# The second head group's square on the other two quadrants of TensorE's array, in turn with the first group's cube

## The chip, the cores and the metric

One core of a Trainium2 chip runs the whole kernel. The metric is the device time of one execution in microseconds (us). The array of TensorE (PE in the profile) has 128 rows and 128 columns; a matmul with a 64x64 stationary operand uses one quadrant of it: its rows are the SBUF partitions of its operands (0 to 63 or 64 to 127), its columns the PSUM partitions of its output. DVE is VectorE, ACT is ScalarE, POOL is GpSimd.

## What is computed

Six stages run over x of 32 batches x 256 tokens x 128, each as x + stage(layernorm(x)): a LoRA feed-forward, linear attention, the feed-forward again, an FP4 feed-forward, Nystrom attention, the FP4 feed-forward again. The change is in the Nystrom stage alone, which computes for each batch and each of 16 heads of 8 dimensions, with 64 landmarks:

```python
kernel1 = softmax(Q @ K_l.T); kernel2 = softmax(Q_l @ K_l.T); kernel3 = softmax(Q_l @ K.T)

def iterative_inv(mat, n_iter=6):
    K = mat
    V = K.T / max(column sums of K)
    for _ in range(n_iter):
        KV = K @ V
        V = (0.25 * V) @ (13 * I - KV @ (15 * I - KV @ (7 * I - KV)))
    return V

out = ((kernel1 @ iterative_inv(kernel2)) @ (kernel3 @ V)) @ w_proj
```

## The kernel before

Each engine runs its own list of instructions in the order in which the program wrote it, and semaphores are the only link between engines. The function `nystrom` writes, for each of the four engines, a loop over blocks: block n holds the six Newton steps of batch n (`run`) and, between them, parts of the batches before it (`tail`, n - 1) and after it (`head`, n + 1, and `fore`, n + 2). The order within a block is written out by hand. Two buffers (`s`, `o`) alternate.

The iteration is kept as a symmetric 64x64 matrix `pm` per head with 8 more columns that carry the product with kernel3 @ V, so that a step is a square and a cube. The 16 heads of a batch lie as 8 pairs: one head of a pair on partitions 0 to 63, the other on 64 to 127. Pairs 0 to 3 are group 0 and pairs 4 to 7 group 1; in PSUM (`pn`) each group fills one bank. For each step `it` and group `g`:

- `multiply` (PE, L1620): 8 matmuls, 64x64 by 64x72, write the square of `pm` to `pn`. The two heads of a pair use the two quadrants on the array's diagonal.
- `square` (ACT, L1378): one instruction copies the group's square, scaled, from `pn` to `sq` in SBUF.
- `remainder` (DVE, L1199): 7 pm - square, with the square read from `pn`, goes to `rm`. POOL's `remainder` (L1471) subtracts `sq` from `pm` into `tm`.
- `cube` (PE, L1630): 8 matmuls of `rm` by `sq` write the product over the square in `pn`, on the same diagonal quadrants.
- `newton` (DVE, L1207): the next `pm` from `pn` and `tm`. In the last step only the 8 extra columns are formed.

Every float32 matmul leaves two MATMUL and two LDWEIGHTS records in the trace, so a group of 8 matmuls is x16 there.

The work between the steps on PE: `turned1` (L1654, L1659), `scores2` (L1540), `back` (L1670), `scores3` (L1553), `turn2` (L1562), `product` (L1680), `totals` (L1690), `turn3` (L1570, four times a block), `columns` (L1576), `project` (L1697), `factors` (L1580), `start_w` (L1590), `turn_w` (L1598), `scores1` (L1640), `turn_x` (L1515), `queries` and `values` (L1522 to L1528), `turn_mx` (L1648) and `start_p` (L1612). `start_p` forms the first `pm` of the next batch: 16 matmuls, 64x64 by 64x64, that go round all four quadrants of the array in turn. DVE also runs row maxima (`max3` L1151, `max1` L1225, `max2` L1136), reciprocals (`invert` L1232), `divide` (L1237) and others; ACT runs the exponentials (`exp3`, L1360) and copies. Where a function is named with numbers, as newton(3,1), they are step and group; turn3(0) is its quarter.

## Time and profile before

| | us |
|---|---|
| median of 3 runs | 2293.45 |
| lowest and highest | 2290.79, 2293.51 |
| the profiled execution, its device time | 2292.12 |
| its span, first to last instruction | 2290.4 |
| the Nystrom stage, its steps L1620 to L1207 | 1052.3 to 2008.2 |

Busy time over the whole span: PE 1966.3 us (86%), PE's weight loads 1526.7, DVE 1718.3 (75%), ACT 1014.1, POOL 707.7. A row of groups gives an engine's instructions of one line: how many, their busy time (overlaps counted once), the mean time of one, and how long the engine sat idle before them, with the one that ended the idle time. Matmuls are pipelined: a group's own time in a row reaches to the end of its last matmul, while the next group starts earlier. The distance between the starts of two rows is therefore what the first one costs the engine.

### The profile page before, as it was taken

What the parts mean: (1) busy time and instruction counts of PE and PEld (TensorE: products, weight loads), DVE (VectorE), ACT (ScalarE), POOL (GpSimd) and SP (SyncE); (2) the same over time, 40 slices, a digit from 0 to 9 for tenths busy, and PEclk for the clock granted to TensorE, in tenths of its full rate; (3) what the DMA queues carried; (4) which work ended last, traced back from release to release, by engine and by line L of the source; (5) the groups of instructions that cost most, each with busy time, mean ns of one, the idle gap of its engine ahead of it and who ended that gap; (6) DMA issues with size and microseconds to landing.
All of it is one profiled execution on the core that took longest, in us unless ns stands there. A gap on an engine that the chain in (4) does not pass through costs nothing.

```text
span 2290.4 us, 66040 instructions
## 1 busy us (share of the span) xinstructions
PE 1966.3 (86%) x27657; PEld 1526.7 (67%) x27657; DVE 1718.3 (75%) x4007; ACT 1014.1 (44%) x2652; POOL 707.7 (31%) x835
## 2 busy tenths in 40 slices
PE   1999888888899677768999999999999999957775
PEld 0888555555688455546778778878887787735553
DVE  5666687787666699975777777777777777669995
ACT  1443222222344454444555555555555555345552
POOL 1000566666000122213333333333333333312221
PEclk9999999999999899988999999999999999979997
DMA  3000000000000000000000000000000000000002
GB/s 105 1 1 1 1 1 1 2 1 2 1 2 1 1 1 1 1 1 2 3 3 3 3 3 3 3 3 3 3 3 3 3 3 3 3 1 0 1 1 74
DMA packets 14551, 14.42 MB, mean 6 GB/s; under 512 B 1392, under 2 KB 12080, under 8 KB 14256
## 3 DMA queue, kind: packets, MB, share of 16 engines
q1 hardware_dynamic: 14256, 10.20, 1.6%
q8 instruction: 220, 3.60, 0.6%
q14 instruction: 75, 0.61, 0.1%
HBM read 6.01 MB, written 4.19 MB: 4 GB/s over the span
## 4 chain that ended last, share of the span: by engine, by line
PE 66%; DVE 21%; POOL 5%; ACT 4%; issue 3%; SPq 0%; DVEq 0%; POOLq 0%; DMA 0%
PE acc L1630 9%; PE acc L1620 9%; PE acc L467 6%; PE acc L444 5%; POOL arena L924 4%; DVE arena L888 3%; DVE arena L881 3%; PE acc L740 3%; PE acc L758 3%; DVE arena L891 3%; ACT arena L937 3%; PE acc L1654 2%; PE acc L458 2%; DVE arena L879 2%; PE acc L1640 2%
## 5 line engine op out<-in xcount | busy, mean ns | idle before, releaser
L1471 POOL TENSOR_TENSOR arena<-arena 128x288 f32<-128x288 f32 (+1 forms) x384 | 266.4, 708 | 484.8 <-ACT arena L1378 484.8
L924 POOL TENSOR_TENSOR arena<-arena 128x960 f32<-128x960 f32 (+2 forms) x70 | 118.1, 1687 | 577.3 <-DVE arena L891 571.8
L1199 DVE SCALAR_TENSOR_TENSOR arena<-arena,acc 128x256 f32<-128x256 f32 x384 | 160.7, 419 | 132.5 <-ACT arena L1378 121.1
L1620 PE MATMUL acc<-arena 64*64 64x72 f32 x6144 | 248.7, 227 | 1.0 <-DVE arena L1207 1.0
L1620 PEld LDWEIGHTS acc<-arena 64*64 64x64 f32 x6144 | 211.2, 133 | 56.4 <-issue 36.8
L1378 ACT ACTIVATE arena<-acc 128x288 f32<-128x288 f32 x384 | 157.9, 412 | 197.7 <-PE acc L1620 182.2
L1630 PE MATMUL acc<-arena 64*64 64x72 f32 x6144 | 241.1, 222 | 3.7 <-DVE arena L1199 3.5
L1630 PEld LDWEIGHTS acc<-arena 64*64 64x64 f32 x6144 | 208.7, 133 | 42.3 <-issue 27.2
L1207 DVE SCALAR_TENSOR_TENSOR arena<-acc,arena 128x288 f32<-128x288 f32 (+1 forms) x384 | 154.8, 410 | 68.4 <-PE acc L1630 57.8
L993 PE MATMUL acc<-wguT,arena 128*128 128x352 f32 x256 | 116.2, 540 | 60.7 <-DVE arena L863 57.2
L419 ACT ACTIVATE arena<-acc,wib 128x256 f32<-128x256 f32 x256 | 100.5, 475 | 150.5 <-PE acc L458 150.5
L1015 PE MATMUL acc<-wdT,arena 128*128 128x128 f32 (+1 forms) x768 | 105.7, 288 | 71.1 <-ACT arena L952 70.4
L662 POOL TENSOR_TENSOR arena<-arena,quadcol 128x512 f32<-128x512 f32 x64 | 65.3, 1042 | 289.9 <-DVE arena L539 289.9
L1015 PEld LDWEIGHTS acc<-wdT,arena 128*128 128x128 f32 (+1 forms) x768 | 93.2, 195 | 86.5 <-ACT arena L952 86.5
L565 DVE TENSOR_TENSOR arena<-acc,tri 128x512 f32<-128x512 f32 x192 | 120.6, 683 | 31.3 <-PE acc L740 31.3
L637 ACT COPY arena<-acc 128x512 f32<-128x512 f32 x64 | 37.6, 588 | 234.2 <-PE acc L740 234.2
L1360 ACT ACTIVATE arena<-acc,arena 128x256 f32<-128x256 f32 x256 | 119.5, 476 | 43.7 <-DVE arena L1151 43.7
L467 PEld LDWEIGHTS acc<-wout,arena 128*128 128x128 f32 x1024 | 119.1, 191 | 22.1 <-issue 22.1
L467 PE MATMUL acc<-wout,arena 128*128 128x128 f32 x1024 | 131.3, 281 | 1.2 <-DVE X L377 1.2
L444 PE MATMUL acc<-arena,wi 128*128 128x256 f32 x512 | 125.2, 389 | 0.0
L942 ACT ACTIVATE arena<-acc 128x352 f32<-128x352 f32 x128 | 58.3, 455 | 131.0 <-PE acc L993 131.0
L937 ACT ACTIVATE arena<-arena 128x960 f32<-128x960 f32 (+2 forms) x70 | 65.5, 935 | 108.8 <-DVE arena L881 108.6
(233 smaller groups left out, 4429.9 us busy)
## 6 DMA issues: line engine op xcount, KB each, us to landing
out_dram<-X SPq DMA_DIRECT2D x4, 1024.0 KB, 9.3
wi<-in_wiT_dram SPq DMA_DIRECT2D x1, 256.0 KB, 2.7
wout<-in_woT_dram SPq DMA_DIRECT2D x1, 256.0 KB, 3.3
wqkv<-in_w_qkv_dram SPq DMA_DIRECT2D x1, 192.0 KB, 2.7
arena<-in_w_down_dram SPq DMA_DIRECT2D x1, 176.0 KB, 2.3
arena<-in_w_gate_dram SPq DMA_DIRECT2D x1, 128.0 KB, 2.1
arena<-in_w_up_dram SPq DMA_DIRECT2D x1, 128.0 KB, 2.3
wq<-in_WqT_dram SPq DMA_DIRECT2D x1, 64.0 KB, 2.2
```

What stands on the lines that cost most here:

```text
L444: pe.matmul(hp[f], wi[:, f * P:(f + 1) * P], xnT[s], start=True, stop=False, skip_group_check=True)
L467: mm = pe.matmul(yp[s][:, j, :], hid[s][:, f, j * P:(j + 1) * P], wout[:, f, :], start=(f == 0), stop=(f == FT - 1), skip_group_check=True)
L565: dve.tensor_tensor(att[s][:, j * NQ + q, :].rearrange("p (h q) -> p h q", q=P), A[q].rearrange("p (h q) -> p h q", q=P), tri[:, 0:P].unsq ...
L924: pool.tensor_tensor(b3(zq[s][:, cols]), b3(rnd[s][:, cols]), each(small[s][:, 1, blocks(n)]), ALU.mult).then_inc(zq_ready, 1)
L937: act.activation(big[s][:, part(n)], y[s][:, part(n)], ACT.Abs, scale=2.0 ** 22)\
L1015: mm = pe.matmul(yp[:, j, :], hqT[s][j][0:w, c, :], wdT[0:w, c, :], start=(c == 0), stop=(c == HT - 1), skip_group_check=True)
L1199: dve.scalar_tensor_tensor(rm[s][:, group[g], :], pm[s][:, group[g], 0:LM], 7.0 * size[it], pn[s][:, group[g], 0:LM], ALU.mult, ALU.subtra ...
L1207: dve.scalar_tensor_tensor(pm[s][:, group[g], cols], pn[s][:, group[g], cols], 1.0 / (15.0 * size[it] ** 2), tm[s][:, group[g], cols], ALU ...
L1378: act.mul(sq[s][:, group[g], :], pn[s][:, group[g], 0:MW], 15.0 / (13.0 * size[it]))\
L1471: pool.tensor_tensor(tm[s][:, group[g], cols], pm[s][:, group[g], cols], sq[s][:, group[g], cols], ALU.subtract).then_inc(tm_ready, 1)
L1620: mm = pe.matmul(pn[s][rows, p, 0:MW], pm[s][rows, p, 0:LM], pm[s][rows, p, :], start=True, stop=True, skip_group_check=True)
L1630: mm = pe.matmul(pn[s][rows, p, cols], rm[s][rows, p, :], sq[s][rows, p, cols], start=True, stop=True, skip_group_check=True)
```

## The change

**Off the diagonal.** Group 1's square is now written to the other half of the partitions: a matmul whose operands lie on partitions 0 to 63 writes to 64 to 127, and the other way round. So it uses the two quadrants off the diagonal. Group 0's square and both cubes stay on the diagonal.

**In turn.** A new function `cross` issues, for p = 0 to 3, the two matmuls of group 0's cube for pair p and then the two of group 1's square for pair 4 + p. `multiply` is left for group 0 and `cube` for group 1. `cross` waits for what both need: `sq` and `rm` of group 0, `pm` of group 1.

**Back in two halves.** ACT copies group 1's square to `sq` with two instructions of 64 partitions each, each to the half where the head belongs. DVE's remainder of group 1 reads the square from `sq` instead of from `pn`, with other factors.

**New order.** All four lists are written anew, so that group 1 runs half a step behind group 0. `scores2` and `max2` move into the next block, ACT's `norm` is issued for n + 3 instead of n + 4. One semaphore for DVE's internal chains replaces one per stage.

```diff
+                    square, lead = (pn[s], 7.0 * size[it]) if g == 0 else (sq[s], 105.0 / 13.0)
+                    dve.scalar_tensor_tensor(rm[s][:, group[g], :], pm[s][:, group[g], 0:LM], lead,
+                                             square[:, group[g], 0:LM], ALU.mult, ALU.subtract).then_inc(rm_ready, 1)
...
+                    part = 1.0 / (15.0 * size[it] ** 2) if g == 0 else 13.0 / (225.0 * size[it])
...
                 def square(n, s, it, g):
                     act.wait_ge(sq_done, step(n, it, g))
-                    act.mul(sq[s][:, group[g], :], pn[s][:, group[g], 0:MW], 15.0 / (13.0 * size[it]))\
-                       .then_inc(sq_ready, 1)
+                    part = 15.0 / (13.0 * size[it])
+                    if g == 0:
+                        ins = act.mul(sq[s][:, group[g], :], pn[s][:, group[g], 0:MW], part)
+                    else:
+
+                        for (rows, _), (other, _) in zip(halves, halves[::-1]):
+                            ins = act.mul(sq[s][rows, group[g], :], pn[s][other, group[g], 0:MW], part)
+                    ins.then_inc(sq_ready, 1)
...
+                def cross(n, s, it):
+
+                    cols = slice(LM if it == NITER - 1 else 0, MW)
+                    pe.wait_ge(sq_ready, step(n, it, 0))
+                    pe.wait_ge(rm_ready, step(n, it, 0))
+                    iterate(pe, n, it, 1)
+                    for p in range(PG):
+                        for rows, _ in halves:
+                            mm = pe.matmul(pn[s][rows, p, cols], rm[s][rows, p, :], sq[s][rows, p, cols],
+                                           start=True, stop=True, skip_group_check=True)
+                        if p == PG - 1:
+                            mm.then_inc(cube_done, 1)
+                        r = PG + p
+                        for (rows, _), (other, _) in zip(halves, halves[::-1]):
+                            mm = pe.matmul(pn[s][other, r, 0:MW], pm[s][rows, r, 0:LM], pm[s][rows, r, :], start=True,
+                                           stop=True, skip_group_check=True)
+                    mm.then_inc(sq_done, 1)
```

PE's list after it, in a full block, is: multiply(0), turned1, scores2, cube(5,1) of the batch before, cross(0), back, scores3, multiply(1), cube(0,1), product, turn3(0), cross(1), totals, multiply(2), turn3(1), cube(1,1), turn2, turn3(2), cross(2), turn3(3), project, multiply(3), columns, cube(2,1), start_w, cross(3), factors, turn_w, multiply(4), scores1, cube(3,1), turn_x, cross(4), queries, values, multiply(5), turn_mx, start_p, cube(4,1), turned1, cross(5).

The first place is PE from `scores1` on, late in a block. Before, in the names above: scores1, cube(4,0), turn_x, multiply(4,1) with multiply(5,0), queries, values:

```order
L1640 MATMUL acc<-arena 128x256 x8
L1630 MATMUL acc<-arena 64x72 x8
L1515 MATMUL acc<-ident,arena 128x128 x2
L1620 MATMUL acc<-arena 64x72 x16
L1522 MATMUL acc<-arena,wqkv 128x256
L1523 MATMUL acc<-arena,wqkv 128x256
L1528 MATMUL acc<-wqkv,arena 128x128 x2
```

After, L1676 is scores1, L1648 cube(3,1), L1533 turn_x, and L1660 and L1666 are the two matmuls of the cube and the two of the square in `cross`:

```order
L1676 MATMUL acc<-arena 128x256 x8
L1648 MATMUL acc<-arena 64x72 x8
L1533 MATMUL acc<-ident,arena 128x128 x2
L1660 MATMUL acc<-arena 64x72 x2
L1666 MATMUL acc<-arena 64x72 x2
L1660 MATMUL acc<-arena 64x72 x2
L1666 MATMUL acc<-arena 64x72 x2
L1660 MATMUL acc<-arena 64x72 x2
L1666 MATMUL acc<-arena 64x72 x2
```

Between the cube of group 1 and the next `cross` of the same batch only turn_x is left.

The second place is PE from `scores3` (L1553, then L1571) to the first `turn3` (L1570, then L1588), early in a block. Before:

```order
L1553 MATMUL acc<-arena 128x256 x8
L1630 MATMUL acc<-arena 64x72 x16
L1562 MATMUL acc<-ident,arena 128x128 x4
L1680 MATMUL acc<-arena 32x256 x8
L1620 MATMUL acc<-arena 64x72 x16
L1690 MATMUL acc<-arena 32x256 x8
L1570 MATMUL acc<-ident,arena 128x128 x4
```

After, L1638 is multiply(1), L1648 cube(0,1) and L1716 product:

```order
L1571 MATMUL acc<-arena 128x256 x8
L1638 MATMUL acc<-arena 64x72 x8
L1648 MATMUL acc<-arena 64x72 x8
L1716 MATMUL acc<-arena 32x256 x8
L1588 MATMUL acc<-ident,arena 128x128 x4
```

One group of steps, turn2 and totals no longer stand between scores3 and turn3(0).

The third place is DVE in the middle of a block, from `divide` (L1237, then L1244) on. Before, L1161 to L1166 are `largest`, L1242 and L1246 `finish`:

```order
L1237 TENSOR_TENSOR arena<-acc,arena 128x256
L1161 TENSOR_REDUCE arena<-acc 8x2
L1164 RECIPROCAL arena<-arena 8x2
L1166 TENSOR_TENSOR arena<-arena,tsel 8x8
L1199 SCALAR_TENSOR_TENSOR arena<-arena,acc 128x256
L1242 SCALAR_TENSOR_TENSOR X<-acc,X 128x256
L1246 BN_STATS bn<-X 128x6 x2
L1171 COPY arena<-acc 128x8
L1207 SCALAR_TENSOR_TENSOR arena<-acc,arena 128x288
L1199 SCALAR_TENSOR_TENSOR arena<-arena,acc 128x256 x2
```

After, L1214 is newton, L1161 `columns`, and L1205 a remainder: with arena alone as its source it is group 1's, with arena and acc (PSUM) group 0's:

```order
L1244 TENSOR_TENSOR arena<-acc,arena 128x256
L1214 SCALAR_TENSOR_TENSOR arena<-acc,arena 128x288
L1161 TENSOR_REDUCE arena<-arena 128x4x2
L1205 SCALAR_TENSOR_TENSOR arena<-arena 128x256
L1249 SCALAR_TENSOR_TENSOR X<-acc,X 128x256
L1253 BN_STATS bn<-X 128x6 x2
L1205 SCALAR_TENSOR_TENSOR arena<-arena,acc 128x256
L1214 SCALAR_TENSOR_TENSOR arena<-acc,arena 128x288
L1166 TENSOR_REDUCE arena<-acc 8x2
```

The remainders of the two groups no longer follow each other, and group 1's has both sources in SBUF.

## Rows read from the trace of the kernel before

**Rows 1.** Busy time in windows: start:end, length, engines, clock, DMA share, GB/s.

```profile
core 0: us, PE busy (x) PEld busy (x) DVE busy (x) ACT busy (x) POOL busy (x), PEclk, DMA share, GB/s
1400.00:1600.00 200.00, 198.95 (x4191) 160.88 (x4187) 152.71 (x359) 110.00 (x288) 73.86 (x107) 1.00 0.01 3
```

**Rows 2.** One line's instructions: turn_mx (L1648) between 1400 and 1600 us.

```profile
L1648 PE MATMUL acc<-ident,arena x7: 327/327/328, 1406.4 to 1586.6; 128*128 128x128 f32 x7
```

**Rows 3.** Timeline of PE over one block: start, us, line, records.

```profile
start us, us, engine line op out<-in xcount [idle before <-releaser]
...
1505.19 1.20 PE L1620 MATMUL acc<-arena 64*64 64x72 f32 x32
1506.32 1.15 PE L1553 MATMUL acc<-arena 32*128 32x256 f32 x16
1507.40 1.22 PE L1630 MATMUL acc<-arena 64*64 64x72 f32 x32
1508.55 0.66 PE L1562 MATMUL acc<-ident,arena 128*128 128x128 f32 x4
1509.13 1.07 PE L1680 MATMUL acc<-arena 128*32 128x256 f32 x16
1510.13 1.22 PE L1620 MATMUL acc<-arena 64*64 64x72 f32 x32
...
1512.28 0.66 PE L1570 MATMUL acc<-ident,arena 128*128 128x128 f32 x4
...
1515.14 0.72 PE L1620 MATMUL acc<-arena 64*64 64x72 f32 x16
1516.04 0.71 PE L1697 MATMUL acc<-wproj,arena 128*128 128x128 f32 x4 [0.18 <-DVE arena L1237]
...
1517.12 0.38 PE L1580 MATMUL acc<-arena,hsel 8*128 8x8 f32 x2
1517.43 0.72 PE L1620 MATMUL acc<-arena 64*64 64x72 f32 x16
...
1520.73 0.44 PE L1598 MATMUL acc<-ident,arena 128*128 128x128 f32 x2
1521.09 1.15 PE L1640 MATMUL acc<-arena 32*128 32x256 f32 x16
1522.17 0.72 PE L1630 MATMUL acc<-arena 64*64 64x72 f32 x16
1522.82 0.44 PE L1515 MATMUL acc<-ident,arena 128*128 128x128 f32 x2
1523.18 1.22 PE L1620 MATMUL acc<-arena 64*64 64x72 f32 x32
1524.33 0.70 PE L1522 MATMUL acc<-arena,wqkv 128*128 128x256 f32 x2
...
1527.12 0.27 PE L1612 MATMUL acc<-arena 64*64 64x64 f32 x1
...
1527.23 0.67 PE L1612 MATMUL acc<-arena 64*64 64x64 f32 x30
1527.82 0.71 PE L1654 MATMUL acc<-arena 32*128 32x256 f32 x8
```

**Rows 4.** Timeline of PE where the stage begins.

```profile
1049.04 1.13 PE L1612 MATMUL acc<-arena 64*64 64x64 f32 x32 [0.55 <-ACT arena L1350]
...
1052.27 2.19 PE L1620 MATMUL acc<-arena 64*64 64x72 f32 x32
```

**Rows 5.** Busy time in windows, of these two rows.

```profile
1049.00:1050.20 1.20, 1.13 (x32) 0.97 (x32) 0.04 (x1) 0.68 (x2) 1.08 (x2) 0.50 0.00 0
1052.20:1054.40 2.20, 2.20 (x34) 1.97 (x32) 1.04 (x2) 0.41 (x1) 0.31 (x1) 0.50 0.00 0
```

**Rows 6.** Timeline of ACT: two copies out of PSUM, back to back.

```profile
1525.50 0.38 ACT L1345 ACTIVATE arena<-acc 128x256 f32<-128x256 f32 x1 [0.64 <-PE acc L1523]
1525.78 0.37 ACT L1346 COPY arena<-acc 128x256 f32<-128x256 f32 x1
```

**Rows 7.** Groups by line in the stage: count, busy us, mean ns, idle before.

```profile
L1199 DVE SCALAR_TENSOR_TENSOR arena<-arena,acc 128x256 f32<-128x256 f32 x384 | 160.7, 419 | 132.5 <-ACT arena L1378 121.1 <-issue 0.3
L1378 ACT ACTIVATE arena<-acc 128x288 f32<-128x288 f32 x384 | 157.9, 412 | 197.7 <-PE acc L1620 182.2
L1360 ACT ACTIVATE arena<-acc,arena 128x256 f32<-128x256 f32 x248 | 115.7, 476 | 42.2 <-DVE arena L1151 42.2
L1151 DVE TENSOR_REDUCE arena<-acc 128x2 f32<-128x512 f32 x124 | 79.5, 681 | 3.5
```

**Rows 8.** Timeline of all engines: newton and the PE groups around it.

```profile
1517.98 0.67 PE L1630 MATMUL acc<-arena 64*64 64x72 f32 x16
...
1518.69 0.46 DVE L1207 SCALAR_TENSOR_TENSOR arena<-acc,arena 128x288 f32<-128x288 f32 x1 [0.89 <-PE acc L1630]
```

**Rows 9.** Timeline of all engines in the FP4 stage that follows.

```profile
2027.89 0.42 DVE L891 SCALAR_TENSOR_TENSOR arena<-arena 128x256 f32<-128x256 f32 x1
2028.23 0.42 DVE L888 SCALAR_TENSOR_TENSOR arena<-arena 128x256 f32<-128x256 f32 x1
2028.39 0.73 POOL L924 TENSOR_TENSOR arena<-arena 128x256 f32<-128x256 f32 x1 [1.90 <-DVE arena L891]
...
2028.68 0.73 DVE L891 SCALAR_TENSOR_TENSOR arena<-arena 128x256 f32<-128x256 f32 x1
...
2029.55 0.62 POOL L924 TENSOR_TENSOR arena<-arena 128x256 f32<-128x256 f32 x1 [0.43 <-DVE arena L891]
```

More of the change, by code:

```diff
@@ L340, in v @@
             def v(dve):
-                chain = Chain(dve, steps)
+                chain = links.on(dve)
                 def norm(n, s):
@@ L534, in v @@
             def v(dve):
-                chain = Chain(dve, steps)
+                chain = links.on(dve)
                 def queries(n, s):
@@ L847, in v @@
             def v(dve):
-                chain = Chain(dve, steps)
+                chain = links.on(dve)
                 def finish(n):
@@ L1126, in v @@
             def v(dve):
-                chain = Chain(dve, steps)
+                chain = links.on(dve)
                 def landmarks(n, s):
@@ L1279, in v @@
                     if run:
+                        remainder(n, s, 1, 0)
+                        newton(n, s, 0, 1)
+                    if head:
+                        kernel2(n + 1, o)
+                        max3(n + 1, o, 2)
+                    if run:
                         newton(n, s, 1, 0)
-                        newton(n, s, 1, 1)
                     if head:
-                        max3(n + 1, o, 2)
                         max3(n + 1, o, 3)
-                        columns(n + 1, o)
                     if run:
-                        remainder(n, s, 2, 0)
-                        remainder(n, s, 2, 1)
+                        remainder(n, s, 1, 1)
                     if tail:
@@ L1291, in v @@
                     if run:
-                        newton(n, s, 2, 0)
-                        newton(n, s, 2, 1)
+                        remainder(n, s, 2, 0)
+                        newton(n, s, 1, 1)
                     if tail:
                         invert(n - 1, o, 1)
+                        divide(n - 1, o)
+                    if run:
+                        newton(n, s, 2, 0)
+                    if head:
+                        columns(n + 1, o)
+                    if run:
+                        remainder(n, s, 2, 1)
                     if tail:
-                        divide(n - 1, o)
+                        finish(n - 1, o)
+                    if run:
+                        remainder(n, s, 3, 0)
+                        newton(n, s, 2, 1)
                     if head:
@@ L1433, in a @@
                     if run:
+                        square(n, s, 3, 1)
                         square(n, s, 4, 0)
+                    if far:
+                        norm(n + 3, o)
                     if fore:
@@ L1443, in a @@
                     if run:
+                        square(n, s, 5, 0)
                         turned_mx(n, s)
-                    if fore and n + 4 < NB:
-                        norm(n + 4, s)
-                    if run:
                         square(n, s, 5, 1)
@@ L1721, in t @@
                     if run:
-                        cube(n, s, 1, 0)
+                        multiply(n, s, 1, 0)
+                        cube(n, s, 0, 1)
+                    if tail:
+                        product(n - 1, o)
+                    if head:
+                        turn3(n + 1, o, 0)
+                    if run:
+                        cross(n, s, 1)
+                    if tail:
+                        totals(n - 1, o)
+                    if run:
+                        multiply(n, s, 2, 0)
+                    if head:
+                        turn3(n + 1, o, 1)
+                    if run:
                         cube(n, s, 1, 1)
@@ L1725, in t @@
                         turn2(n + 1, o)
+                        turn3(n + 1, o, 2)
+                    if run:
+                        cross(n, s, 2)
+                    if head:
+                        turn3(n + 1, o, 3)
                     if tail:
-                        product(n - 1, o)
+                        project(n - 1, o)
                     if run:
-                        multiply(n, s, 2, 0)
-                        multiply(n, s, 2, 1)
-                    if tail:
-                        totals(n - 1, o)
-                    if head:
-                        turn3(n + 1, o, 0)
-                    if run:
-                        cube(n, s, 2, 0)
-                        cube(n, s, 2, 1)
-                    if head:
-                        turn3(n + 1, o, 1)
-                    if head:
-                        turn3(n + 1, o, 2)
+                        multiply(n, s, 3, 0)
                     if head:
@@ L1744, in t @@
                     if run:
-                        multiply(n, s, 3, 0)
-                    if tail:
-                        project(n - 1, o)
-                    if head:
-                        turn3(n + 1, o, 3)
-                        factors(n + 1, o)
-                    if run:
-                        multiply(n, s, 3, 1)
-                        cube(n, s, 3, 0)
+                        cube(n, s, 2, 1)
                     if head:
@@ L1778, in t @@
                     if run:
+                        cube(n, s, 4, 1)
                         turned1(n, s, 0)
-                        multiply(n, s, 5, 1)
-                    if fore:
-                        scores2(n + 2, s)
+                        cross(n, s, 5)
             vec.append(v), ten.append(t), sca.append(a), gps.append(g)
```

122 lines of the change are left out of this document (56 added, 66 removed).

## The prediction

> **What bounds the kernel now.** I read busy time in windows first, then one block of PE's timeline, then the groups by line. In the Nystrom stage PE is busy 198.95 of 200 us at the full clock (1.00, which is 2.4 GHz); DVE is busy 152.71, ACT 110.00, POOL 73.86 [rows 1]. A block takes (1586.6 - 1406.4) / 6 = 30.03 us, by the start of the one turn_mx in each of seven blocks [rows 2], so 32 blocks are 961 us of the 2290.4. "Busy" could hide waiting, since a matmul's record lasts longer than it holds the engine. So see the distances between starts: they repeat the same few values. Two groups of eight matmuls in a row, 32 records, cost 1523.18 to 1524.33 = 1.15 us; one group alone, 1522.17 to 1522.82, costs 0.65 [rows 3]. So a group costs 0.50 us, and each run of one tile shape costs 0.15 once, for the change of shape. Only one group is longer than that: multiply(3,0), 1515.14 to 1516.04 = 0.90, because `project` waits for DVE's `divide`, 0.25 us [rows 3]. PE's own throughput therefore sets the block, and what leaves PE leaves the time, as long as the other engines keep up.
>
> **What the change removes: the time of six groups of matmuls.** In each of the six steps, `cross` puts the 8 matmuls of a cube on the diagonal quadrants between the 8 of a square off the diagonal. Before, these are two groups at 0.50 us each. Does the array run four quadrants together? The trace has one operation that goes round all four, `start_p`. At the full clock its 32 records run from 1527.12 to the next group at 1527.82: 0.70, less 0.15 for the change of shape, 0.55 us [rows 3]. On the diagonal, 32 records of a group pair cost 1.00. The stage's beginning shows the same without neighbours: 32 records in 1.13 us on four quadrants against 32 in 2.19 us on two [rows 4], both at clock 0.50, which is 1.2 GHz [rows 5]. The columns differ a little, 64 against 72. So four quadrants do run together, and a `cross` costs between 0.50 (all 16 matmuls in the time of 8) and 0.55 x 72 / 64 = 0.62. I take the middle, 0.56: `start_p` is slowed at its head by the cube's last 8-column matmuls, which `cross` mostly isn't. Removed: 6 x (1.00 - 0.56) = 2.64 us a block; between the ends, 2.28 to 3.00.
>
> The banks are the one thing that `start_p` doesn't show in this form: there each half of the rows writes to one bank, here each half writes to both, at different output partitions. The pairs on the diagonal already write one bank from both halves at this pace, so I price it at nothing.
>
> The Trainium skill has a rule against this: TensorE: Matmul & The Clock Gate, Part 3 (The mechanism), says that a weight load overlaps running matmuls only when it goes to another row group, and the two quadrants of one half of the partitions share theirs. By that rule a `cross` would cost about its two groups, and nothing would be gained; `start_p` contradicts it here.
>
> **What it adds on PE.** Shape changes: counting runs of one tile shape over a block, I get 30 before and 33 after (scores2 now follows turned1 and has the cube behind it; each multiply and each cube of group 1 stands alone; cross(5) and the next multiply(0) share a run). 3 x 0.15 = 0.45 us; at least nothing, if neighbours that aren't 64x64 change more cheaply.
>
> **Stalls.** Group 1 now runs half a step behind, so every dependency has PE work over it. I laid the block out with the costs above and looked for the shortest covers. (a) `cross(4)` needs newton(3,1), which needs cube(3,1), and only turn_x lies between. Cover: 0.65 + 0.36 (turn_x, 1522.82 to 1523.18 [rows 3]) = 1.01. Needed: the cube to the end of its last record 0.72 [rows 3], 0.04 to DVE (1518.65 to 1518.69), newton 0.46 [rows 8], and as much back, 1.26. Stall 0.25 us. (b) `project` now has turn3(3) before it as cover, 0.44 us more, so its 0.25 goes. (c) turn3(0) came 1512.28 - 1506.32 = 5.96 us after scores3; now it comes after scores3 1.08, one run of two groups 1.15 and product 1.00 = 3.23 [rows 3]. In between lie: scores3 to its end 1.15, max3 0.68 and two exponentials of 0.48 [rows 7], with 0.04 at each of three steps: 2.91. But ACT first has the copy for multiply(1,0), which is there 1.08 + 0.72 + 0.04 = 1.84 after scores3 and ends at 2.25; then the exponentials end at 3.21, just in time. No stall, and no reserve. (d) `cross` to the next multiply: 0.56, its last record's end 0.22 later (0.72 - 0.50), newton 0.46 and twice 0.04 = 1.32, against a cover of 0.71 + 0.31 (factors) + 0.36 (turn_w) = 1.38 at the shortest [rows 3].
>
> **On ACT.** 192 more instructions. Back to back, a copy out of PSUM follows after 0.28 us one that lasts 0.38 [rows 6], so a second half of equal length costs about 0.3 each; if 64 partitions were quicker, less. Six a block are 1.8 us on an engine busy 16.5 of 30; between a `cross` and the cube(it,1) after it stand three groups of other PE work or more, some 2 us and over, which hides them.
>
> **On DVE and POOL.** The number of instructions doesn't change, 22.9 us of busy time a block; of 27.8 that is 82%. But group 1's remainder now has two sources in SBUF. The FP4 stage shows what that does beside POOL: L891, two SBUF sources, 128x256, takes 0.42 us alone and 0.73 while POOL's L924 runs, and that one takes 0.73 instead of 0.62 [rows 9]. Before, the remainder (one source in PSUM) takes 0.419 on average, always with POOL beside it [rows 7]. After, both engines start on the same copy of ACT, so nearly each of the 192 meets POOL's: DVE late by up to 0.31, or POOL by about as much. What I laid out has 0.2 us and more over it at each cube of group 1, except that cube(2,1) is just reached. I price it at nothing and keep it for the second case.
>
> The Trainium skill says the same as these rows: SBUF — State Buffer, Who interferes with whom, has a DVE instruction with two SBUF inputs contend with a GpSimd instruction that reads SBUF, and the second to issue waits for all of the first. By that a remainder that comes just after POOL's (0.8 us) would be late by up to 0.8, not 0.31; the sum would move only where that reaches a cube.
>
> **Elsewhere.** The one semaphore for all chains changes no wait. At the stage's two ends fewer things overlap; norm for n + 3 and scores2 a block later keep the chain of dependencies as it was. I allow 3 us either way.
>
> **The sum.** 30.03 - 2.64 + 0.45 + 0.25 - 0.25 = 27.84 us a block, 2.19 less; 32 blocks: 70.1 us. The profiled execution took 2292.1 and would take 2222.0. The median of the three runs is 1.3 higher, so 2223.
>
> **The rivals.**
> - Short covers (0.20). PE waits for DVE or ACT in places that I took as covered: the remainder of group 1 beside POOL, turn3(0) without reserve, DVE's maxima (0.68 and 1.2 us each) standing ahead of a newton. If 0.31 at each of the six remainders reached PE, that is 1.86 a block: 29.70, and 2283. Half of it gives 2253. For: DVE at 82%, in order, and PE's list with covers of 0.0 to 0.3 in (c) and at cube(2,1). Against: group 1 has several PE groups over it in most steps.
> - No gain (0.04). The chain of six steps, or DVE's list, is so tight that the block stays at 30: 2289 to 2297. Against: DVE's 22.9 us leave five, and group 1's loop (`cross` 0.56 and 0.22, two halves on ACT 0.65, remainder 0.42, the 1.26 of (a), 0.04 three times) is 3.23 us, six of them 19.4.
> - Slower (0.09). The quadrants of one half don't overlap in this order, or two halves writing two banks at once hold each other up. Then a `cross` costs 1.00 and the new shape changes are added: 30.03 + 0.45 = 30.48, 14 us more, 2308. It decides itself at `cross` = 1.00 - 0.45 / 6 = 0.93 us: above that the kernel is slower than before. The rule above about weight loads leads here. Against: `start_p` on four quadrants at 0.55, and 1.13 against 2.19 at the slow clock.
>
> **The numbers.** The forecast has 0.67. Its own range is 2204 (`cross` at 0.50, six times 0.06 less, and one of the shape changes cheaper, 0.5 us a block, 17 us) to 2245 (`cross` at 0.62 and 0.3 us of small stalls a block, 21 us). To leave out no more than 2 in 10, the range takes in the lower two thirds of the short covers: 2202 to 2264. A difference under 0.2% (4.6 us) can't be told from none. Faster by more: 0.67 + 0.20 = 0.87; within: 0.04; slower: 0.09.
>
> **What would show it.** In the profile after: the distance from the first record of a `cross` to the next group should be 0.65 to 0.77 (with the change of shape); turn_mx should come each 27.8 us; the remainder of group 1 should have a mean above 0.42, up to 0.73; ACT's copies of group 1 should come in pairs, 0.3 us between their starts. PE should wait about 0.25 us before `cross(4)` and nowhere else by more than 0.1. The prediction is wrong if a `cross` costs 0.9 or more, or if PE's idle time per block grows beyond 1 us.

## The result and the profile after

The changed kernel takes 2227.78 us (median of 4 runs, 2226.31 to 2232.23), the kernel before in the same comparison 2293.26: a ratio of 0.972, 95% interval 0.9703 to 0.9737. The forecast was 2223 us with a range of 2202 to 2264. The profiled execution of the changed kernel has a span of 2225.7 us, where that of before has 2290.4, 64.7 more.

Where the time went can be read from the one turn_mx of each block, over all 32 of them (one line's instructions in each kernel; L1648 before, L1684 after):

```profile
L1648 PE MATMUL acc<-ident,arena x32: 327/327/329, 1076.0 to 2002.1; 128*128 128x128 f32 x32
```

```profile
L1684 PE MATMUL acc<-ident,arena x32: 327/328/473, 1069.6 to 1938.7; 128*128 128x128 f32 x32
```

The 31 distances sum to 926.1 us before and 869.1 after: 57.0 of the 64.7 us lie there. Another 6.4 lie ahead of the first turn_mx and 1.3 behind the last. In the steady part, one line's instructions between 1100 and 1320 us of the kernel after:

```profile
L1684 PE MATMUL acc<-ident,arena x7: 327/328/329, 1125.8 to 1294.1; 128*128 128x128 f32 x7
```

A block takes (1294.1 - 1125.8) / 6 = 28.05 us, against 30.03 [rows 2]. Busy time in a window, which answers to [rows 1]:

```profile
core 0: us, PE busy (x) PEld busy (x) DVE busy (x) ACT busy (x) POOL busy (x), PEclk, DMA share, GB/s
1400.00:1600.00 200.00, 195.28 (x4422) 152.81 (x4421) 166.02 (x388) 132.71 (x355) 85.77 (x114) 1.00 0.01 3
```

PE is no longer busy all the time (195.28 of 200 us instead of 198.95), and DVE has come to 83%. One `cross` in PE's timeline, between turn3(0) (L1588) and totals (L1726); L1660 is the cube, L1666 the square:

```profile
start us, us, engine line op out<-in xcount [idle before <-releaser]
...
1417.43 0.66 PE L1588 MATMUL acc<-ident,arena 128*128 128x128 f32 x4
1418.02 0.28 PE L1660 MATMUL acc<-arena 64*64 64x72 f32 x2
1418.03 0.28 PE L1666 MATMUL acc<-arena 64*64 64x72 f32 x2
1418.13 0.23 PE L1660 MATMUL acc<-arena 64*64 64x72 f32 x2
...
1418.50 0.23 PE L1660 MATMUL acc<-arena 64*64 64x72 f32 x2
1418.52 0.23 PE L1666 MATMUL acc<-arena 64*64 64x72 f32 x2
1418.68 1.07 PE L1726 MATMUL acc<-arena 128*32 128x256 f32 x16
```

In this `cross` the square's records start some 0.01 us after the cube's, and the whole of 32 records costs 1418.02 to 1418.68 = 0.66 us, of which 0.15 is the change of shape: 0.51. It costs what one group of 8 matmuls cost before. The two waits of PE in a block are before cube(2,1) and before cross(4):

```profile
1424.93 0.27 PE L1594 MATMUL acc<-ident,arena 128*8 128x128 f32 x1
1425.59 0.72 PE L1648 MATMUL acc<-arena 64*64 64x72 f32 x16 [0.40 <-DVE arena L1205]
...
1430.31 0.72 PE L1648 MATMUL acc<-arena 64*64 64x72 f32 x16
1430.96 0.44 PE L1533 MATMUL acc<-ident,arena 128*128 128x128 f32 x2
1431.68 0.28 PE L1660 MATMUL acc<-arena 64*64 64x72 f32 x2 [0.28 <-DVE arena L1214]
```

From `columns` (L1594) to cube(2,1) it is 0.66 us, and from turn_x (L1533) to cross(4) 0.72. Without a wait the two distances are 0.20 (e1 below) and 0.36 (1522.82 to 1523.18 [rows 3]), so the waits cost 0.46 and 0.36 us. The number in brackets, idle time, is smaller because the records before them last longer than they hold the engine. What the first waits for, in the timeline of DVE and of POOL at that moment:

```profile
1423.81 0.68 DVE L1161 TENSOR_REDUCE arena<-arena 128x8 f32<-128x512 f32 x1
1424.40 1.05 DVE L1205 SCALAR_TENSOR_TENSOR arena<-arena 128x256 f32<-128x256 f32 x1
...
1424.37 0.80 POOL L1488 TENSOR_TENSOR arena<-arena 128x288 f32<-128x288 f32 x1 [2.42 <-ACT arena L1395]
```

DVE's remainder begins 0.03 us after POOL's and takes 1.05 us instead of 0.42; it ends 0.28 after POOL's has ended. All 192 remainders of group 1 overlap one of POOL. In 93 of them POOL began first, and each of these ends 0.28 us after POOL's, whatever its start (they last 0.45 to 1.05). In the other 99 DVE began first; it takes 0.41 to 0.43, and POOL's instruction is the longer one, mostly 1.04 instead of 0.80. By shape over the stage, the remainder of group 1 (SBUF alone) and of group 0 (acc is PSUM), which answers to [rows 7]:

```profile
L1205 DVE SCALAR_TENSOR_TENSOR arena<-arena 128x256 f32<-128x256 f32 x192 | 108.9, 567 | 43.0 <-ACT arena L1395 41.9
L1205 DVE SCALAR_TENSOR_TENSOR arena<-arena,acc 128x256 f32<-128x256 f32 x192 | 79.9, 416 | 6.8 <-ACT arena L1391 3.8
```

### The profile page after: what moved, and what is told of

Same layout as the page of the kernel before. It is cut to its first block, busy times and chain, and to the rows that moved or that the text cites. A ratio compares the mean times of both kernels' runs of the same rounds, so it can differ in the third digit from the quotient of the medians.

```text
span 2225.7 us, 66232 instructions
## 1 busy us (share of the span) xinstructions
PE 1885.5 (85%) x27657; PEld 1441.6 (65%) x27657; DVE 1729.8 (78%) x4007; ACT 1077.4 (48%) x2844; POOL 738.2 (33%) x835
## 4 chain that ended last, share of the span: by engine, by line
PE 61%; DVE 24%; POOL 5%; ACT 4%; issue 4%; SPq 0%; DVEq 0%; POOLq 0%; DMA 0%
PE acc L472 6%; PE acc L449 5%; PE acc L1648 5%; PE acc L1638 4%; POOL arena L929 4%; PE acc L1660 3%; DVE arena L893 3%; DVE arena L886 3%; PE acc L745 3%; PE acc L763 3%; DVE arena L896 3%; ACT arena L942 3%; PE acc L1690 2%; PE acc L463 2%; PE acc L1588 2%
## 5 line engine op out<-in xcount | busy, mean ns | idle before, releaser
L1488 POOL TENSOR_TENSOR arena<-arena 128x288 f32<-128x288 f32 (+1 forms) x384 | 292.9, 769 | 454.9 <-ACT arena L1395 399.8
L1395 ACT ACTIVATE arena<-acc 64x288 f32<-64x288 f32 x384 | 155.6, 405 | 139.7 <-PE acc L1666 132.3
L1214 DVE SCALAR_TENSOR_TENSOR arena<-acc,arena 128x288 f32<-128x288 f32 (+1 forms) x384 | 156.7, 408 | 68.8 <-PE acc L1660 38.1
L1648 PE MATMUL acc<-arena 64*64 64x72 f32 (+1 forms) x3072 | 133.2, 223 | 13.5 <-DVE arena L1205 13.2
L1660 PE MATMUL acc<-arena 64*64 64x72 f32 (+1 forms) x3072 | 134.5, 224 | 11.8 <-DVE arena L1214 11.6
L1205 DVE SCALAR_TENSOR_TENSOR arena<-arena 128x256 f32<-128x256 f32 x192 | 108.9, 567 | 43.0 <-ACT arena L1395 41.9
L1648 PEld LDWEIGHTS acc<-arena 64*64 64x64 f32 x3072 | 111.0, 133 | 46.5 <-issue 44.4
L1638 PE MATMUL acc<-arena 64*64 64x72 f32 x3072 | 137.5, 229 | 3.4 <-DVE arena L1214 2.5
L1660 PEld LDWEIGHTS acc<-arena 64*64 64x64 f32 x3072 | 109.7, 133 | 46.3 <-issue 40.4
L1666 PE MATMUL acc<-arena 64*64 64x72 f32 x3072 | 138.5, 229 | 0.0
L1638 PEld LDWEIGHTS acc<-arena 64*64 64x64 f32 x3072 | 109.7, 133 | 40.1 <-DVE arena L1214 21.6
```

The lines of the kernel that those rows point to most:

```text
L1214: dve.scalar_tensor_tensor(pm[s][:, group[g], cols], pn[s][:, group[g], cols], part, tm[s][:, group[g], cols], ALU.mult, ALU.add).then_inc ...
L1395: ins = act.mul(sq[s][rows, group[g], :], pn[s][other, group[g], 0:MW], part)
L1488: pool.tensor_tensor(tm[s][:, group[g], cols], pm[s][:, group[g], cols], sq[s][:, group[g], cols], ALU.subtract).then_inc(tm_ready, 1)
L1638: mm = pe.matmul(pn[s][rows, p, 0:MW], pm[s][rows, p, 0:LM], pm[s][rows, p, :], start=True, stop=True, skip_group_check=True)
L1648: mm = pe.matmul(pn[s][rows, p, cols], rm[s][rows, p, :], sq[s][rows, p, cols], start=True, stop=True, skip_group_check=True)
L1660: mm = pe.matmul(pn[s][rows, p, cols], rm[s][rows, p, :], sq[s][rows, p, cols], start=True, stop=True, skip_group_check=True)
```

## The experiments

Each experiment takes a part of the change away or moves one thing. The ratio is to the kernel before in the same comparison (its median was 2291.8 to 2293.3 us). "A block" is the mean distance of turn_mx between 1100 and 1320 us in the profile of each.

| kernel | us, median | ratio to before (95% interval) | a block, us |
|---|---|---|---|
| before | 2293.26 | | 30.03 |
| after | 2227.78 | 0.972 (0.9703 to 0.9737) | 28.05 |
| e1: square back on the diagonal | 2305.03 | 1.0054 (1.0039 to 1.0069) | 30.49 |
| e2: cube, then square | 2255.95 | 0.9844 (0.9828 to 0.9861) | 29.05 |
| e3: POOL second, all steps | 2212.44 | 0.9656 (0.9642 to 0.9671) | 27.64 |
| e4: group 0 in halves too | 2248.57 | 0.9814 (0.9799 to 0.9828) | 28.66 |
| e5: cube(2,1) before columns | 2222.13 | 0.9699 (0.9686 to 0.9712) | 27.87 |
| e7: and cube(3,1) before scores1 | 2221.35 | 0.9689 (0.9676 to 0.9702) | 27.83 |
| e8: and POOL second | 2221.51 | 0.9693 (0.9677 to 0.9708) | 27.85 |
| e9: before, off the diagonal only | 2291.52 | 0.9994 (0.9985 to 1.0003) | 29.84 |
| e10: e3, scores1 in two parts | 2208.81 | 0.9636 (0.9623 to 0.9649) | 27.49 |
| e11: POOL second, step 2 only | 2214.23 | 0.9658 (0.9645 to 0.9671) | 27.64 |

**e1: is it the quadrants?**

```diff
-                            mm = pe.matmul(pn[s][other, r, 0:MW], pm[s][rows, r, 0:LM], pm[s][rows, r, :], start=True,
+                            mm = pe.matmul(pn[s][rows, r, 0:MW], pm[s][rows, r, 0:LM], pm[s][rows, r, :], start=True,
...
-                            ins = act.mul(sq[s][rows, group[g], :], pn[s][other, group[g], 0:MW], part)
+                            ins = act.mul(sq[s][rows, group[g], :], pn[s][rows, group[g], 0:MW], part)
```

> The changed kernel with one thing undone: group 1's square goes back to the quadrants on the diagonal (ACT's two half copies then keep each half on its side); order, turns, half copies and the remainder from SBUF stay. Theory A (the gain is the time that the four quadrants share): a cross costs 1.0 us again instead of 0.51, 6 x 0.49 = 2.94 us a block more, of which the two waits seen after (0.36 before cross(4), 0.41 before cube(2,1)) may swallow up to 0.77: a block of 30.2 to 31.0 us, 2296 to 2322 us in all. Theory B (the gain comes from the new order, which covers waits better): 28.1 us a block, 2228.

Measured: 2305.03 us, 0.5% slower than before, inside the range of theory A. PE's timeline at `columns` (L1594) and cube(2,1), and at cross(4) of this kernel; L1540 is queries:

```profile
1396.16 0.27 PE L1594 MATMUL acc<-ident,arena 128*8 128x128 f32 x1
1396.37 0.72 PE L1648 MATMUL acc<-arena 64*64 64x72 f32 x16
...
1402.94 0.34 PE L1660 MATMUL acc<-arena 64*64 64x72 f32 x4 [0.28 <-DVE arena L1214]
1403.09 0.32 PE L1666 MATMUL acc<-arena 64*64 64x72 f32 x4
...
1403.71 0.32 PE L1660 MATMUL acc<-arena 64*64 64x72 f32 x4
1403.84 0.32 PE L1666 MATMUL acc<-arena 64*64 64x72 f32 x4
1404.09 0.70 PE L1540 MATMUL acc<-arena,wqkv 128*128 128x256 f32 x2
```

A `cross` costs 1402.94 to 1404.09 = 1.15, less 0.15: 1.00 us. At 0.49 each, six of them are 2.94 us a block more than after; 0.46 of it is taken up by the wait before cube(2,1), which is gone here (0.20 from `columns` instead of 0.66): 28.05 + 2.94 - 0.46 = 30.53, measured 30.49. So without the shared time of the quadrants nothing of the gain is left, and the new order alone is a loss. Theory B falls.

**e2: must they stand in turn?**

```diff
-                        if p == PG - 1:
-                            mm.then_inc(cube_done, 1)
-                        r = PG + p
+                    mm.then_inc(cube_done, 1)
+                    for p in range(PG):
+                        r = PG + p
```

> The changed kernel with cross issuing all 8 matmuls of the cube and then all 8 of the square, still off the diagonal, instead of in turn. Theory A (PE starts matmuls in the order of its list, so quadrants share time only where neighbours in the list use different ones): a cross costs 0.95 to 1.0 us instead of 0.51, a block 30.0 to 31.0, 2290 to 2322 us. Rival (PE finds the free quadrants by itself among what is queued): a cross stays near 0.5 and the time at 2228.

Measured: 2255.95 us, between the two theories; neither is right. PE's timeline of cross(1), and L1726 (totals) after it:

```profile
1426.51 0.53 PE L1660 MATMUL acc<-arena 64*64 64x72 f32 x10
1426.83 0.28 PE L1666 MATMUL acc<-arena 64*64 64x72 f32 x2
...
1427.01 0.54 PE L1666 MATMUL acc<-arena 64*64 64x72 f32 x11
1427.47 1.07 PE L1726 MATMUL acc<-arena 128*32 128x256 f32 x16
```

It costs 1426.51 to 1427.47 = 0.96, less 0.15: 0.81 us. The square's first records start after 10 of the cube's 16, and so they do in each of the 192 crosses of this trace: PE took up a matmul for a free quadrant ahead of three that stand before it in the list, never of more. So two groups in a row keep 0.19 of the 0.49 us, and taking turns brings the other 0.30, at the four crosses that stand between groups of another shape. cross(0) and cross(5) have other 64x64 groups as neighbours, and all stretches of 64x64 matmuls together take 1.4 us a block more than after. The wait before cube(2,1) is gone here too (the one before cross(4) is not), which leaves the 1.00 us of 29.05 - 28.05. The Trainium skill (TensorE: Matmul & The Clock Gate, Part 3, The mechanism) has matmuls start and end strictly in the order of the list; between quadrants this trace shows otherwise, by six records.

**e9: the other quadrants in the old order.** Before's kernel with group 1's square off the diagonal, its half copies and its remainder from SBUF, as in the diff of the change, without `cross` and without the new order.

```diff
-                        for rows, _ in halves:
-                            mm = pe.matmul(pn[s][rows, p, 0:MW], pm[s][rows, p, 0:LM], pm[s][rows, p, :], start=True,
+                        for (rows, _), (other, _) in zip(halves, halves[::-1] if g else halves):
+                            mm = pe.matmul(pn[s][other, p, 0:MW], pm[s][rows, p, 0:LM], pm[s][rows, p, :], start=True,
```

> The kernel before, in its own order, with only group 1's square off the diagonal, its copy back in two halves and its remainder from SBUF: no turns, no cross. Theory A (what brings the time is that neighbours in PE's list use different quadrants; without turns only the border of two groups overlaps, 0.19 us each as in e2): five borders between a square of group 1 and a group on the diagonal save up to 0.95 us a block, less what the half copies (0.42 us later for group 1) and POOL's and DVE's shared reads cost in an order that was not made for them: a block of 29.1 to 30.0 us, 2263 to 2292 us. Rival (using the other quadrants alone, wherever, gives the gain): near 2230.

Measured: 2291.52 us, no difference from before, at the upper end of theory A. PE's timeline shows both sides: two squares (L1627) at 0.96 instead of 1.15 where a change of shape follows, and cube(1,1) late, because it waits for its remainder (L1200 is DVE's):

```profile
1420.51 1.03 PE L1627 MATMUL acc<-arena 64*64 64x72 f32 x32
1421.47 1.07 PE L1697 MATMUL acc<-arena 128*32 128x256 f32 x16
```

```profile
1417.39 0.72 PE L1637 MATMUL acc<-arena 64*64 64x72 f32 x16
1418.28 0.72 PE L1637 MATMUL acc<-arena 64*64 64x72 f32 x16 [0.17 <-DVE arena L1200]
1418.93 0.66 PE L1569 MATMUL acc<-ident,arena 128*128 128x128 f32 x4
```

The pair of cubes takes 1.54 instead of 1.15. Five borders save 0.95 us a block, and 0.19 is left (30.03 to 29.84). Three waits take the rest: 0.39 at cube(1,1), 0.20 between cube(4,1) and turn_mx (1405.82 to 1406.66 = 0.84 instead of 0.64), and 0.16 from there to cube(5,0) (1407.08, 0.42 instead of 0.26). At cube(1,1) the remainder began late, behind the half copies, and took 0.65 beside POOL instead of 0.42; how much each of the two costs in this order was not tried alone. The other quadrants gain nothing in the old order, and the new order nothing without them (e1): the gain needs both.

**e3 and e11: DVE's remainder beside POOL's.** POOL waits until DVE's remainder of the same group is done; in e11 with `if g and it == 2`.

```diff
                     pool.wait_ge(sq_ready, step(n, it, g))
+                    if g:
+                        pool.wait_ge(rm_ready, step(n, it, g))
```

> The changed kernel with POOL's remainder of group 1 waiting for DVE's remainder of group 1, so that the two never run together. Theory A (after, DVE's remainder of group 1 takes 0.567 us on average and up to 1.05 because POOL's remainder reads SBUF at the same time, and that makes the wait of 0.41 us before cube(2,1)): the mean falls to about 0.42, the distance from columns to cube(2,1) on PE from 0.66 to about 0.25 to 0.35, a block from 28.06 to about 27.7, 2216 us; POOL's later end costs nothing, since newton of group 1 comes over 0.5 us after it. Rival (cube(2,1) is late because DVE's list has divide, newton and columns before the remainder, POOL beside it doesn't matter): mean and distance stay, 2228.

Measured: 2212.44 us, 4 below what theory A expected. The remainder of group 1 by shape, and PE's timeline at columns (L1596) and cube(2,1) (L1650):

```profile
L1205 DVE SCALAR_TENSOR_TENSOR arena<-arena 128x256 f32<-128x256 f32 x192 | 81.2, 423 | 42.8 <-ACT arena L1395 41.7
```

```profile
1392.10 0.27 PE L1596 MATMUL acc<-ident,arena 128*8 128x128 f32 x1
1392.31 0.72 PE L1650 MATMUL acc<-arena 64*64 64x72 f32 x16
```

The mean is 0.423 instead of 0.567, the distance 0.21 instead of 0.66, and the block is shorter by nearly as much, 28.05 to 27.64. No remainder of group 1 overlaps one of POOL any more. A wait was added and the kernel became faster: what the wait settles is who reads SBUF first.

> The changed kernel with POOL waiting for DVE's remainder of group 1 in step 2 alone, instead of in all six as in e3. Theory A (of the six places where the two engines read SBUF together only the remainder of (2,1) reaches PE): the same block as e3, 27.60 us, 2212 us, although the mean of group 1's remainder stays well above 0.42. Rival (the late remainders add up on DVE and e3 gained by all of them): between 2216 and 2228.

Measured: 2214.23 us and the same block as e3, 27.64, though the remainder's mean is still 0.469:

```profile
L1205 DVE SCALAR_TENSOR_TENSOR arena<-arena 128x256 f32<-128x256 f32 x192 | 90.0, 469 | 42.8 <-ACT arena L1395 41.7
```

So of the six places where the two engines meet, the one in step 2 is the one that PE feels. It is also the one with the longest remainder: the mean after is 1.00 us in step 2, 0.65 in step 0 and 0.43 to 0.45 in the others.

**e4: are the half copies hidden?**

```diff
                     if g == 0:
-                        ins = act.mul(sq[s][:, group[g], :], pn[s][:, group[g], 0:MW], part)
+                        for rows, _ in halves:
+                            ins = act.mul(sq[s][rows, group[g], :], pn[s][rows, group[g], 0:MW], part)
```

> The changed kernel with group 0's square too copied back by two instructions of 64 partitions. ACT has 6 x 0.42 = 2.5 us more a block (0.42 each, as group 1's halves stand after: the second starts when the first has ended). Theory A (half copies are hidden as long as their cover is longer): all covers of group 0 but one hold; the exponentials behind square(1,0) come 0.42 later, and turn3(0), which came with no reserve, waits 0.3 to 0.4: a block of 28.4 to 28.5, 2238 to 2243 us. Rival (ACT, busy 66% of the stage, is far from mattering): 2228. If the copies of group 1 were priced in the time as well, each half would show in full: 30.6 us a block, 2308.

Measured: 2248.57 us, 6 above the 2238 to 2243 that theory A expected. PE's timeline between product (L1717) and turn3(0) (L1589):

```profile
1425.49 1.07 PE L1717 MATMUL acc<-arena 128*32 128x256 f32 x16
1427.02 0.66 PE L1589 MATMUL acc<-ident,arena 128*128 128x128 f32 x4 [0.47 <-ACT arena L1371]
```

From product to turn3(0) it is 1.53 us instead of 1.00. The six halves are 2.5 us of ACT's time a block, and the block grows by 0.6: 0.53 before turn3(0), for the exponentials behind the copy, and 0.10 before multiply(3,0), at project, while the wait before cube(2,1) is 0.08 shorter. The place without reserve is where it shows, and the rest is hidden, as theory A says; but that one wait is 0.53 and not 0.3 to 0.4, more than a half copy (0.42).

**e5, e7, e8: other orders around the two waits.** e5:

```diff
                         newton(n, s, 2, 0)
+                        remainder(n, s, 2, 1)
                     if head:
                         columns(n + 1, o)
-                    if run:
-                        remainder(n, s, 2, 1)
...
                         multiply(n, s, 3, 0)
+                        cube(n, s, 2, 1)
                     if head:
                         columns(n + 1, o)
-                    if run:
-                        cube(n, s, 2, 1)
```

> The changed kernel with one pair of neighbours exchanged on two engines: on DVE the remainder of (2,1) comes before columns, on PE cube(2,1) comes before columns. Theory A (the wait of 0.47 us between columns and cube(2,1) is DVE's remainder, which arrives just after POOL's has begun and stands behind it; ahead of columns it would start at the same moment as POOL's or sooner): the wait goes, and multiply(3,0) and cube(2,1) share a run, 0.15 less: a block of 28.06 - 0.47 - 0.15 = 27.44 us, 2208 us. Rival (the wait moves on: start_w or cross(3) then wait for what DVE does later): 28.0 us a block, 2226.

Measured: 2222.13 us: of 20 expected us only 6 came. cube(2,1) comes 0.62 after multiply(3,0), nearly without a wait, but the next groups are late; PE's timeline from columns (L1593) over start_w (L1607) to cross(3):

```profile
1396.00 0.27 PE L1593 MATMUL acc<-ident,arena 128*8 128x128 f32 x1
1396.28 1.07 PE L1607 MATMUL acc<-arena 128*32 128x256 f32 x16
1397.49 0.28 PE L1659 MATMUL acc<-arena 64*64 64x72 f32 x2
```

start_w takes 1.21 instead of 1.00, because cross(3) waits, and `columns` 0.28 instead of 0.20. Of 0.46 + 0.15 = 0.61 us, 0.12 + 0.08 + 0.21 = 0.41 come back, and 0.20 is left, as in the blocks (28.05 to 27.87). The rival holds for the most part. DVE's `columns` now stands behind the remainder and begins 0.40 us after multiply(3,0) (1395.13 against 1394.73), where after has it 0.47 before (1423.81 against 1424.28). That this moves the groups behind it is read from the order of DVE's list; it was not tried alone.

e7 adds cube(3,1) before scores1:

```diff
                         multiply(n, s, 4, 0)
-                        scores1(n, s)
                         cube(n, s, 3, 1)
+                        scores1(n, s)
```

> The kernel of e5 and, in addition, on PE cube(3,1) before scores1, so that scores1 and turn_x (1.45 us) lie between it and cross(4) instead of turn_x alone. Theory A (cross(4) waits 0.36 us for newton(3,1), whose cube is too close): that wait goes and two groups share a run (0.15), but cube(3,1) now waits about 0.35 us for its remainder, which DVE ends 0.35 us after multiply(4,0) leaves PE: 0.15 us a block less than e5, 27.3 us, 2203 us. Rival (a remainder of group 1 costs as much wherever its cube stands, or scores1 later delays DVE's max1 and with it newton(4,0)): 2208 to 2220.

Measured: 2221.35 us, a block of 27.83, above the 2203 of theory A and just above the rival's 2208 to 2220. cross(4) no longer waits (turn_x to queries is 1.03, as in e10 below), but cube(3,1) (L1647) does, behind multiply(4,0) (L1637):

```profile
1399.75 0.72 PE L1637 MATMUL acc<-arena 64*64 64x72 f32 x16
1400.71 0.72 PE L1647 MATMUL acc<-arena 64*64 64x72 f32 x16 [0.25 <-DVE arena L1205]
```

The distance is 0.96 where two groups in a row have 0.50. DVE's remainder is not late here (0.43 us, begun 0.10 after ACT's second half copy), so the wait is for ACT and DVE in turn, and nothing is gained over e5. e8 adds e3's wait on POOL to that:

> The kernel of e7 with POOL's remainder of group 1 waiting for DVE's, as in e3. Theory A (in e5 and e7 the reordering already takes away the one place where the two engines' reads of SBUF reached PE, so the later POOL is worth nothing more): as e7, within 4 us, 2199 to 2207 us. Rival (DVE's remainder of (3,1), on which cube(3,1) now waits, is also held up by POOL): up to 0.3 us a block less than e7, about 2194 us.

Measured: 2221.51 us, the same as e7 within the noise, as theory A said. Its number, 2199 to 2207, rested on e7's and is missed by as much: e7 came out 18 us above its forecast and e5 14.

**e10: the wait before cross(4).** e3's kernel, and scores1 in two parts:

```diff
                         multiply(n, s, 4, 0)
-                        scores1(n, s)
+                        scores1(n, s, 0)
                         cube(n, s, 3, 1)
+                        scores1(n, s, 1)
```

> The kernel of e3 with scores1 in two parts on PE: its first half before cube(3,1), its second half after it. Theory A (the 0.36 us that cross(4) waits is only the short distance from cube(3,1)): the cover grows from 1.01 to about 1.65 us, so the wait of 0.36 goes for one more change of shape at 0.15: a block of 27.60 - 0.21 = 27.4 us, 2206 us. Rival (DVE ends newton(3,1) late anyway, or max1 and newton(4,0) come later for the later scores1 and the next multiply waits): 2212 or above.

Measured: 2208.81 us, the fastest of all. PE's timeline; L1677 is half a scores1, L1650 the cube, L1535 turn_x:

```profile
1396.03 0.71 PE L1677 MATMUL acc<-arena 32*128 32x256 f32 x8
1396.67 0.72 PE L1650 MATMUL acc<-arena 64*64 64x72 f32 x16
1397.32 0.71 PE L1677 MATMUL acc<-arena 32*128 32x256 f32 x8
1397.96 0.44 PE L1535 MATMUL acc<-ident,arena 128*128 128x128 f32 x2
1398.99 0.70 PE L1542 MATMUL acc<-arena,wqkv 128*128 128x256 f32 x2
```

From turn_x to queries it is 1398.99 - 1397.96 = 1.03, which is turn_x 0.37 and `cross` 0.66 and no wait; each half of scores1 costs 0.64. The block is 27.49 against e3's 27.64: 0.15 of the expected 0.21. Over the kernel this is 3.6 us, and the 95% intervals of the two ratios overlap. That the wait went is shown; that e10 is faster than e3 rests on the blocks of one profile each.

## Why the prediction was right

The mechanism was right: the quadrants share their time as forecast, and e1 takes the whole gain away. The forecast block was 27.84 us, the measured one 28.05; the forecast total 2223, the measured 2228. Step by step:

- **The price of a cross** (forecast 0.56, bounds 0.50 to 0.62): 0.51, so 6 x 0.49 = 2.94 us removed a block instead of 2.64. The reading of `start_p`, and of its run at the lower clock on four quadrants against two [rows 3, 4], was right. The middle of the bounds was 0.05 too high: with 72 columns too, 16 matmuls on four quadrants cost what 8 cost on two. The two banks, priced at nothing, cost nothing either. e1 shows the other end, 1.00.
- **Shape changes** (0.45): miscounted by one. By the tile shapes recorded in the traces a block has 31 runs before and 33 after, not 30 and 33. The 0.15 each was not tried alone; the one added in e10 costs (0.64 + 0.64) - 1.08 = 0.20. What the two terms make together is firmer: all stretches of 64x64 matmuls with their changes of shape take 15.25 us of a block before (without the wait at project) and 12.65 after, 2.60 less, and PE's other work 0.05 more. That is 2.55 net, where the forecast has 2.64 - 0.45 = 2.19.
- **Wait (a), before cross(4)** (0.25): 0.36. What was mis-sized is the way back from DVE to PE. Newton ends at 1431.08 + 0.46 = 1431.54 and `cross` starts at 1431.68, 0.14 us, where I had taken the 0.04 of the way from PE to DVE. The newton(3,1) of this block:

```profile
1431.08 0.46 DVE L1214 SCALAR_TENSOR_TENSOR arena<-acc,arena 128x288 f32<-128x288 f32 x1 [0.26 <-PE acc L1648]
```

- **Wait (b), project** (-0.25): gone, as forecast: project (L1733) follows turn3(3) after 0.50 us, without a wait.
- **(c), turn3(0) without reserve**: no wait, product costs 1.00; e4 shows that there was none to spare.
- **The remainder of group 1 beside POOL** (0.31 late at most, priced at nothing): this is the term that was missing. The mechanism was named, and the place, but its size was wrong: up to 0.63 late (1.05 instead of 0.42), and at cube(2,1), "just reached", 0.46 us of it arrive at PE. It was in the rival of the short covers, of whose 1.86 us it is a quarter. The 0.73 of [rows 9] was that of an instruction that began 0.29 us after POOL's, and so late in it; it too ends 0.29 after POOL's (2029.12 to 2029.41). The Trainium skill (SBUF — State Buffer, Who interferes with whom) has the second wait for all of the first, which by the prediction's reading would have given up to 0.8. The trace agrees that the second comes out only behind the first (0.28 us after its end, 93 times of 93), but the most that is lost is 0.63. That the remainder of before always had POOL beside it was a misreading, though a harmless one: 323 of the 384 had, and they take 0.42 as the others do.
- **The half copies** (0.3 us each on ACT, hidden): 0.42 each. Neither of PE's two waits ends with one, so they are hidden, as far as the trace shows; no run has group 1 without them.
- **The ends of the stage** (3 us either way): 64.7 - 32 x 1.98 = 1.3 us more than the blocks explain, within it. In part this is luck, since two larger differences stand against each other. The time ahead of the first turn_mx and behind the last is 7.7 us shorter, where one block's share would be 2.0. The 31 distances are 57.0 shorter instead of 31 x 1.98 = 61.4, because the last of them is 26.32 us after and 25.59 before, and several others are up to 0.41 longer than the rest.

The sum in the prediction's terms with what was measured: 30.03 - 2.94 + 0.45 - 0.25 + 0.36 + 0.46 = 28.11, against 28.05; with 2.55 net for the first two terms, 28.05. A too high price of `cross` (0.30 us a block) stood against waits that were too small (0.57 us in two places). That the total came within 5 us, nearer than either of these errors over 32 blocks (10 and 18 us), is partly luck. The lower end of the forecast's own range also has a slip: 2223 less the 17 us named there is 2206, not 2204, which changes nothing. Of the signs that the prediction named, two did not come: PE waits at a second place by more than 0.1 us, cube(2,1), and ACT's copies of group 1 stand 0.42 apart and not 0.3. PE's waits come to 0.82 us a block, under the 1 us that was named as the sign of being wrong.

The rivals of no gain and of slower did not happen. The rule on weight loads, which led to the slower one, would have made a `cross` cost two groups; it cost 0.51. e1 is what the slower rival would have looked like, 2305 for a forecast of 2308.

## What to carry to other kernels

Where matmuls of 64x64 leave half of the array idle, put independent ones on the other two quadrants and write them in turn: here 16 cost what 8 did. It paid only together with an order that gave the later group half a step of cover; in the old order three waits took the gain back (e9). Before moving an operand of a DVE instruction from PSUM to SBUF, look for what GpSimd reads at that moment: here the one that began second always ended behind the other, and an added wait that settled who goes first was worth 15 us. When an engine stops being the bound, write down the cover of each dependency as it is laid out; the ones at zero are where the next change shows.

## What the runs showed of the hardware

- A copy of 64x288 by ACT takes as long as one of 128x288 (0.41 us), and the second half starts 0.42 after the first in all 192 pairs: 1409.68 to the next instruction at 1410.53 for two. The copies of [rows 6], 128x256, follow each other after 0.28 though one lasts 0.38. It is the same in e1, where the halves stay on their side. Whether the 64 partitions are the reason was not tried.

```profile
1409.68 0.82 ACT L1395 ACTIVATE arena<-acc 64x288 f32<-64x288 f32 x2 [2.57 <-PE acc L1666]
1410.53 0.41 ACT L1391 ACTIVATE arena<-acc 128x288 f32<-128x288 f32 x1
```

- PE started a matmul for an idle quadrant ahead of up to three (six records) that stand before it in its list (e2), so that even groups in a row share some time: 0.19 us a border, in e2 and in e9.
- A DVE instruction with two sources in SBUF and a POOL instruction that reads SBUF: the one that begins second is the one that is delayed. DVE as the second ended 0.28 us after POOL's end, 93 times of 93 in the kernel after; with one source in PSUM DVE took 0.42 beside POOL too.
- From DVE's end to PE's start it is 0.14 us at cross(4) and at cube(2,1) (1425.45 to 1425.59), about three times the way from PE to DVE.
